# A graph-attention and expert layer on one core: GpSimd's fourteen gathers of a step in seven pairs, each behind a signal of VectorE

## What is computed

```python
x = x + gnn(layernorm(x))
x = x + ffn(layernorm(x))
# gnn
h = (x @ W).reshape(n, 4, 64)
alpha = leaky_relu(a_src[src] + a_dst[dst], 0.2)
amax = segment_max(alpha, dst)
alpha = exp(alpha - amax[dst])
alpha = alpha / (segment_sum(alpha, dst)[dst] + 1e-16)
out = segment_sum(alpha[:, :, None] * h[src], dst)
out = relu(layernorm(out + bias) * gamma + beta)
# ffn: mean of all rows -> router -> two experts; each gelu(x @ W1) @ W2, weighted sum, layernorm
```

## Time and profile before

| | us |
|---|---|
| median of 3 runs | 4384.11 |
| lowest and highest run | 4333.09, 4386.15 |
| profiled execution | 4346.76 |
| its span, first to last instruction | 4345.1 |
| VectorE busy in it | 2306.0 (53%) |
| TensorE busy in it | 2490.8 (57%) |
| GpSimd busy in it | 1621.1 (37%) |
| ScalarE busy in it | 1524.8 (35%) |

### The profile page before, as it was taken

The page is one execution under the profiler, slowest core; times in us unless marked ns, Lnnn a source line. Parts: engine busy times, 40 slices in busy tenths (PEclk is TensorE's granted clock), DMA queues, the critical chain, the costliest instruction groups (busy, mean ns, idle before and its releaser), DMA issues. The chain is left out here.

```text
span 4345.1 us, 63198 instructions
## 1 busy us (share of the span) xinstructions
PE 2490.8 (57%) x12486; PEld 1752.7 (40%) x12486; DVE 2306.0 (53%) x9734; ACT 1524.8 (35%) x4803; POOL 1621.1 (37%) x1686
## 2 busy tenths in 40 slices
PE   8344445444554444444455444544455456999999
PEld 6233333333333333333333333333333344666666
DVE  6255455545555544555555544554555555665556
ACT  5233333333333333333333333333333342222221
POOL 0544554445444444444444444444444420000000
PEclk9666666666666667666666666666666667999999
DMA  6534343333433343334333343333433331111111
GB/s 202 173 102 118 113 120 114 110 117 116 118 115 115 117 121 107 113 114 122 113 116 113 114 120 111 113 112 115 118 117 114 112 100 39 39 35 33 39 39 36
DMA packets 236663, 453.66 MB, mean 104 GB/s; under 512 B 57559, under 2 KB 167149, under 8 KB 236461
## 3 DMA queue, kind: packets, MB, share of 16 engines
q0 software_dynamic: 80096, 229.59, 19.9%
q1 hardware_dynamic: 155158, 221.25, 15.3%
q10 hardware_dynamic: 1207, 1.09, 0.1%
HBM read 408.77 MB, written 43.00 MB: 104 GB/s over the span
## 5 line engine op out<-in xcount | busy, mean ns | idle before, releaser
L610 POOL DMA_INDIRECT rows<-table,idx x1666 | 1614.4, 969 | 1784.7 <-DVE o L1365 938.9
L705 PE MATMUL bank<-msg,oh 128*128 128x260 f32 x3332 | 1038.5, 477 | 0.8 <-DVE num L1307 0.5
L718 PE MATMUL bank<-ident_b,ohT 128*128 128x128 bf16 x1666 | 196.8, 309 | 1255.8 <-DVE ohT L1163 828.3
L705 PEld LDWEIGHTS bank<-msg,oh 128*128 128x128 f32 x3332 | 788.6, 244 | 159.5 <-DVE num L1307 1.4
L718 PEld LDWEIGHTS bank<-ident_b,ohT 128*128 128x128 bf16 x1666 | 165.9, 143 | 1303.2 <-issue 740.2
L1219 DVE TENSOR_REDUCE edge_v<-bank 128x112 f32<-128x336 f32 x119 | 60.4, 508 | 1186.2 <-remote 1049.3
L940 ACT ACTIVATE bank<-le 128x56 f32<-128x56 f32 x119 | 26.3, 221 | 1377.7 <-DVE le L1262 502.8
L913 ACT ACTIVATE msg<-rows,we 128x65 f32<-128x65 f32 x1904 | 468.2, 344 | 0.1
L1170 DVE TENSOR_TENSOR msg<-rows,bank 128x520 f32<-128x520 f32 x595 | 395.3, 680 | 0.8 <-ACT bank L940 0.4
L805 PE MATMUL bank<-rows,msg 128*128 128x256 f32 x1536 | 340.6, 378 | 0.0
L792 PE MATMUL bank<-rows 128*128 128x512 f32 x768 | 337.0, 596 | 4.4 <-DMA rows<-in_L_ffn_W 4.4
(11 more groups left out here) (198 smaller groups left out, 3533.0 us busy)
## 6 DMA issues: line engine op xcount, KB each, us to landing
dst_b<-in_dst SPq DMA_DIRECT2D x121, 896.0 KB
rows<-table,idx POOLq DMA_INDIRECT x1666
tab_w<-table SPq DMA_DIRECT2D x121, 134.5 KB
x_w<-in_x_rows SPq DMA_DIRECT2D x121, 128.0 KB
x_mid<-x_o SPq DMA_DIRECT2D x119, 128.0 KB
table<-msg SPq DMA_DIRECT2D x50, 269.0 KB, 3.0
rows<-x_mid SPq DMA_DIRECT2D x26, 512.0 KB, 3.8
msg<-in_x_rows SPq DMA_DIRECT2D x51, 256.0 KB, 3.1
```

The costliest lines, as they stand in the source:

```text
L610: pool.indirect_dma_start(rows[:, slot, t, :], None, table, bass.IndirectOffsetOnAxis(ap=idx[slot][:, t:t + 1], axis=0), bounds_check=None ...
L705: mm = pe.matmul(psA, oh[:, of, t, :], msg[:, of, t, :], start=(t == 0), stop=(t == TILES - 1))
L718: mm = pe.transpose(ps[:, c:c + P], ohT[:, q, t, :], ident_b[:, :])
```

## The change

The order of GpSimd's gathers stays, and so do the four waits ahead of them. Ahead of every second gather comes one more wait, for a signal of VectorE of two steps before, and one more `hold`:

```diff
@@ -322,6 +322,7 @@
             MNODE* AD* MAXSELF* xmid ZN* SHIFT* st_m HI* REST* MID* mv_m LO*""", 6)
+        PACE = ["EDGE_V", "ohT*", "merged3", "num3", "biased3", "normed", "st_m"]
         act2 = Ticks(sem("act2"), """oh ln2 y2 lhs rexp we we_act carried acc asrc* oh_b* wself msgs0 msgs carry ln1 y1""", 6)
@@ -607,6 +608,9 @@
                 dve2.wait(pool, MSGS[-1], at, -3)
                 hold(pool, s_granted)
                 for t in range(TILES):
+                    if t % 2 == 0:
+                        dve2.wait(pool, PACE[t // 2], at, -2)
+                        hold(pool, s_granted)
                     pool.indirect_dma_start(rows[:, slot, t, :], None, table,
                                             bass.IndirectOffsetOnAxis(ap=idx[slot][:, t:t + 1], axis=0),
                                             bounds_check=None, oob_is_err=False).then_inc(s_rows[slot], 16)
```

## The result

| | before | after |
|---|---|---|
| median | 4385.13 us (4 runs) | 3752.16 us (4 runs) |
| lowest and highest | 4333.09, 4388.1 | 3743.9, 3754.66 |
| profiled execution's span | 4345.1 | 3753.0 |
| VectorE busy | 2306.0 (53%) | 2309.4 (62%) |
| GpSimd busy | 1621.1 (37%) | 1597.4 (43%) |

The ratio is 0.8575, with a 95% interval of 0.8519 to 0.863. I had forecast 4100 us, a gain of 284; it was 633. The experiments then added what neither time tells. The runs behind them landed on six chips, with the kernel before beside them each time. On three of these (called A, B and C here) it took 4363, 4615 and 4583 us; on the other three (D, E, F) 3064 to 3068. On D and on F the changed kernel takes the time of the kernel before, to within 0.2%. Which chip the table's runs were on isn't noted; by their times it is one of the first kind, nearest to A, and so are the profiles of before and after.

The account below looks back on a forecast made before the run. Gathers in flight were taken to delay TensorE's signals, so VectorE waits. Per step 16.5 + 6.3 + 3.6 = 26.4 us against 28.7, over 115 steps, gave 4100 us; the range holding 8 in 10 was 3600 to 4700.

Parts of the forecast that it names:

- What bound the kernel: VectorE waits at line 1219 for TensorE's "expand", whose signal comes late while gathers are in flight; a step takes 28.7 us.
- the shadow: Stretch in which TensorE's signals and SyncE's instructions come late: 2.7 to 3.7 us behind a gather's start, closed at 1.25 us spacing.
- The change adds and removes nothing: Same fourteen gathers and bytes; seven waits and increments on GpSimd's queue, at most 1.4 us a step, fit in its idle time.
- The base of the sum, 16.5 us: Length of an undisturbed step, read from the steps at the end with no gathers left.
- Line 718 (722) on time: TensorE's transposes, issued 2.9 to 3.9 us into the step, taken as ahead of the late stretch from 4.0: no loss.
- my slower rival: Pairs 0 and 1 catch line 718, some 5 us lost, 4660 us; decides from a loss of 2.3 us there; chance 0.30.
- Line 1359 (1363), 6.3 us: Line 752's matmuls at 9.4 fall in a gapless late stretch to 16.3, so line 1359 starts at 16.5, not 10.2.
- Line 1219 (1223), 3.6 us: "Half" on time, "expand" inside the last pairs' late stretch and released at 26.4 instead of 22.8: 3.6 us lost.
- Two gathers are too few: Rival: pairs make nothing late, GpSimd bounds the step at 18 us, 3120 us; chance 0.20 for below 3700.
- GpSimd busy over 85%: Sign, over the stage with TensorE waits gone, that pairs are too short to delay TensorE and GpSimd bounds the step.
- The stall is not the gathers' doing: Rival: line 1219's signal is late for a reason that stays, so seven waits change nothing: 4300 to 4470 us; chance 0.16.

Follow-up runs that it names:

- e1: Kernel before without the walk's gathers and the two waits for their rows, on chip A: 2935.11 us, ratio 0.6724.
- e15: Kernel before, ring slots filled in turn by usual gathers, gathers of 64 floats, plain SyncE DMAs, gathers of 32 rows, on chip B: 4186.19 us, ratio 0.9074.
- e16: Changed kernel, ring slots in turn not filled, by seven gather pairs, plain SyncE DMAs, one gather run, on chip C: 3764.46 us, 0.8209 to kernel before.
- e4: Kernel before with seven of the fourteen "expand" matmuls (line 690) left out in the loop, on chip A: 4265.34 us, ratio 0.9772.
- e8: Changed kernel with two waits in place of seven, four gathers behind SEL* and ten behind num3, on chip D: 3066.12 us, ratio 1.0003.
- e18: Two waits in place of seven again, four gathers behind SEL* and ten behind num3, on chip F: 3069.25 us, 1.0001 to kernel before.

## Why the prediction was half right

**What bound the kernel: right, for these chips.** TensorE's signals and SyncE's instructions are late while gathers are in flight; e1 shows it (there lines 490 and 475 of SyncE, which are 492 and 475 before, are 1.2 us apart again, 1005.67 and 1006.88). I called the stretch the shadow of gathers "in flight"; e15 shows that it goes with GpSimd's gather instructions and not with what they carry, and e16 that plain DMAs of the same bytes don't do it.

**The change adds and removes nothing: right.** GpSimd's busy time is 1597.4 us against 1621.1 and the new waits are not seen on the chips of the second kind (1.0003 and 1.0007).

**The base of the sum, 16.5 us: near.** e1 has 16.9, in which VectorE waits 111.4 / 115 = 1.0 us a step as its loop turns and 0.8 at `edge_v`. (A slip that changes nothing: the gathers of the start end at 217.4, not 217.7.)

**Line 718 (722) on time: the step that failed first.** I let the transposes at 2.9 to 3.9 us pass, since the shadow of a gather at 1.3 begins at 4.0. I had put this term at nothing. They were caught in most steps: VectorE waits 298.2 / 87 = 3.4 us at `runmax`, 2.9 a step over all. That is the place of my slower rival, at 3.4 us and not the 5 I gave it, above the 2.3 from which I had said it decides. The time did not come out slower because the next term shrank by more.

**Line 1359 (1363), 6.3 us: the term that was mis-sized, and it more than made up for the first.** I had the shadow go on without a gap from pair 0 to pair 4. But the lateness at `runmax` moves `num3` back, pair 3 leaves at 11.3 us behind `edge_v` (1639.64 - 1628.37) and no longer at 8.8, and the shadow opens: the last gather ahead started at 1636.00, its stretch closed at 1639.7, the next began at 1642.3, and the matmuls of line 756 stand at 1641.20 to 1641.74. `node_v` waits 90.5 / 89 = 1.0 us in such steps, and 1.9 over all, where I had 6.3: this is the term that made the miss. In 17 steps it waited for 103.7 / 17 = 6.1 us: there my course was taken nearly to the letter, with no wait at `runmax` (1.0 us in the first of them). The trace shows what is different in these:

```profile
466.65 0.97 POOL L614 DMA_INDIRECT rows<-table,idx  x1 [2.53 <-DVE sel L1250]
...
469.19 0.94 POOL L614 DMA_INDIRECT rows<-table,idx  x1 [1.58 <-DVE msg L1174]
...
470.38 0.42 DVE L1298 TENSOR_TENSOR_SCAN runmax<-pen,bank 70x128 f32<-70x128 f32 x1
```

In 19 of the 115 steps GpSimd's second gather starts 2.55 us behind the first, in the other 96 by 1.25 to 1.41; the 19 are the steps without a wait at `runmax`, all of them and no others. In e16, on chip C, the same holds: in 7 of the 29 steps with pairs the second gather starts 3.20 us behind the first, and `runmax` is on time in these 7 alone. So a gather with none close behind it lets the transposes through, a pair almost never does (the walk's first step, with 1.0 us at `runmax`, is the one exception). I had read the stretch's edges from the first and last gather of a run and given them to every gather. No run sends single gathers by design, and why the second one is late in these steps stays open. They were not cheaper for it, 24.7 us against 23.4, since `node_v` was then caught.

The signal-paced gathers correct themselves: a delay of VectorE holds the next pair back, which is what I had written against the slower rival and then not put into my own sum.

**Line 1219 (1223), 3.6 us: 1.5 measured.** It waits 2.3 us a step, of which e1 has 0.8 too. I had "half" on time and "expand" caught. By the counter that was so in at least 42 of the 115 steps; in others, as in the one shown, "half" was caught and "expand" came 0.2 us behind it.

In all it is 6.7 us a step over e1's 16.9, where I had 9.9 over 16.5. Put into the sum: 16.9 + 2.9 + 1.9 + 1.5 = 23.2, and VectorE is busy 0.4 us a step more than in e1: 23.6, as measured, against 26.4 forecast; 2.8 us x 115 = 320 us is nearly the whole miss of 348. The direction was right; of the terms, one wait was left out (2.9) and two were put too high (by 4.4 and 2.1). The wait left out is larger than the 2.3 from which I had said that the slower rival decides, so the right direction is in part luck.

**The rivals.** "Two gathers are too few" is wrong on the first kind of chip, where pairs still cost 6.7 us; its time, 3120, is near on the second (3065), and its bound, GpSimd, is right there. Its sign, GpSimd busy over 85%, could not have shown: in gathers back to back only 0.95 of each 1.25 us counts as busy, and on D it is 1570.42 / 2062.10 = 76%. "The stall is not the gathers' doing", for which I had quoted the Trainium skill (SBUF — State Buffer, Who interferes with whom), is refuted by e1. Of the two sentences drawn on, that DMA never contends with a compute engine agrees with the plain DMAs of e16, which held nothing up. That TensorE waits for nobody can't be carried over to when its signals come, which was 10 us late in the profile of before; the page speaks of SBUF's ports, and no run here shows whether a port has a part in this. What the prediction could not know from one trace is that other chips don't have the stall.

## What to carry to other kernels

Before a schedule is tuned around signals that come late for no reason in the program, take the kernel to a second and a third chip: 30 to 34% of this one's time was there on three chips and absent on three. Where the stall is, GpSimd's gathers are better sent a few at a time (3752 us in twos, 3882 in fours, 4224 in one run at the same place), behind marks of the engine that waits for the late signals, since such marks give way when it is late; it cost nothing where the stall isn't. In a sum over paced work, move every later mark by the delays already found before the next one is judged.

## What the runs showed of the hardware

- Six chips, two kinds: the kernel before takes 3064 to 3068 us on three and 4363, 4583 and 4615 us on three. Without gathers it takes 2935 and 2927 us on one of each. D and F were of their kind on two occasions each, and no chip was met in both kinds; that it is the chip and not something around it (its host, or what ran beside it) is not shown.
- On the first kind, a run of fourteen GpSimd gathers holds TensorE's signals up by 10 us (profile of before) to 15.6 and 15.8 us (C, B), and with them SyncE's instructions, whatever the gathers carry (15.80 us for 32 rows each, 15.75 for 128).
- In the profile of before and in e4 (A) TensorE then gets on at one matmul in 0.6 to 0.8 us, and SyncE's instructions stand as far apart (2013.87, 2014.60, 2015.33, 2016.07 around line 475; 0.3 or less at the stage's end). On B and C the line that reads "expand" is released some 3.5 us behind the start of the last gather instead, so no rate by count can be read there.
- A gather with none close behind it (the next 2.55 us later, 3.20 on C) let the fourteen transposes through in 19 of 19 steps, and 7 of 7 on C; two that stood 1.25 to 1.41 us apart did so in 1 of 96, and 0 of 22 on C.
- GpSimd keeps its pace there (a gather every 1.25 us on both kinds of chip), and SyncE's plain DMAs of the same bytes hold up neither SyncE (fourteen in 6.51 us) nor TensorE's signal beside them (at most 0.02 us behind its end in 28 steps on C).
- A gather of 32 rows takes GpSimd 0.863 us, one of 128 rows 0.947 (medians of one step each in e15).
- Left open: what differs between the chips, and by which path a gather reaches TensorE's and SyncE's sequencers and not the others'. No run here looks into that. Nor was the placement of e8 and e18 met by a chip on which it could have mattered.
